# A language-model tower on one core: output products regrouped, and both routers' second products taken over 128 rows

## The reference

```
h = tok(x)                                  # rows of an 8000 x 192 table
h = h + rwkv(layernorm(h))                  # k, v, r = mixed x @ W.T; decayed sums; (sr * y) @ Wo.T
h = h + moe_attention_ffn(layernorm(h))     # router: logits = x @ w_router.T, 4 experts, top 256 of 512 rows each
h = h + ssm_block(layernorm(h))
h = h + experts(layernorm(h))               # router: x @ Wr, 8 experts, top 2, capacity; shared + routed
```

## Time and profile before

| | |
|---|---|
| median of 3 runs | 2166.76 us (2166.21 to 2169.19) |
| the profiled execution: its span, first to last instruction | 2137.2 us |
| the median less that span | 29.6 us |
| TensorE (PE) matmuls busy | 1949.3 us, 91% of the span |
| VectorE (DVE) busy | 1140.4 us, 53% |
| ScalarE (ACT) busy | 739.9 us, 35% |
| GpSimd (POOL) busy | 426.2 us, 20% |
| mean granted TensorE clock | 0.938 |
| the front up to the last copy of logits | 263 us |
| the experts' phase up to its copy of logits | 1365 to 1428 us |

### The profile page before, as it was taken

How to read it: one execution, slowest core, us unless ns; L and a number is a source line. 1 busy time by engine, 2 the same in 40 slices (tenths; PEclk the granted TensorE clock), 3 DMA queues, 4 the chain that set the end, 5 groups by cost and what they waited for, 6 DMA issues and landing times. The chain is left out here.

```text
span 2137.2 us, 28059 instructions
## 1 busy us (share of the span) xinstructions
PE 1949.3 (91%) x10067; PEld 1227.5 (57%) x10075; DVE 1140.4 (53%) x2776; ACT 739.9 (35%) x1248; POOL 426.2 (20%) x567
## 2 busy tenths in 40 slices
PE   4998629999999999879999998799999999999997
PEld 2343523344444544445666665465558888888886
DVE  5798567676667665456877785347322222222221
ACT  1434102544555455544556553121111111111111
POOL 5200111120222021111111111100551222222222
PEclk9988558999999999978999999699999999999999
DMA  2610002111111111000000000200222322122321
GB/s 63 223 50 0 0 18 81 53 52 53 45 53 53 52 45 52 1 31 6 6 6 6 11 6 1 100 1 1 77 95 61 69 60 59 32 62 61 69 38 18
DMA packets 68748, 94.75 MB, mean 44 GB/s; under 512 B 15386, under 2 KB 57662, under 8 KB 66337
## 3 DMA queue, kind: packets, MB, share of 16 engines
q1 hardware_dynamic: 52482, 77.19, 11.2%
q0 software_dynamic: 16128, 15.76, 4.3%
HBM read 54.96 MB, written 39.47 MB: 44 GB/s over the span
## 5 line engine op out<-in xcount | busy, mean ns | idle before, releaser
L1020 DVE TENSOR_REDUCE row_max<-c_ps_m 128x1 f32<-128x512 f32 x384 | 253.1, 686 | 113.8 <-PE c_ps_m L1190 108.5
L1368 ACT ACTIVATE e<-c_ps_s 128x512 f32<-128x512 f32 x384 | 216.5, 596 | 222.2 <-PE c_ps_s L1206 221.5
L2667 DVE TENSOR_TENSOR e_f<-e_ps_u,e_gate 128x512 f32<-128x512 f32 x120 | 83.0, 692 | 271.2 <-ACT e_gate L2949 179.1
L2468 POOL DMA_INDIRECT out<-m_o,m_row_of x80 | 125.7, 1571 | 282.0 <-issue 252.9
L2884 PE MATMUL e_ps_o<-m_w,e_f 128*128 128x192 f32 x960 | 162.6, 326 | 0.9 <-DVE e_f L2667 0.9
L1190 PE MATMUL c_ps_m<-c_kT,qT 96*128 96x512 bf16 x384 | 150.4, 398 | 10.7 <-DVE row_max L1020 10.0
L2884 PEld LDWEIGHTS e_ps_o<-m_w,e_f 128*128 128x128 f32 x960 | 158.1, 190 | 3.3 <-DVE e_f L2667 1.3
L1206 PE MATMUL c_ps_s<-qT,c_kT 97*128 97x512 bf16 x384 | 145.2, 389 | 12.7 <-ACT e L1368 5.3
L2949 ACT ACTIVATE e_gate<-e_ps_g 128x512 f32<-128x512 f32 x120 | 71.6, 597 | 242.3 <-PE e_ps_g L2858 162.3
L2852 PE MATMUL e_ps_g<-m_xT,m_w 128*128 128x256 f32 x480 | 129.6, 392 | 1.0 <-DVE h L2499 1.0
L2852 PE MATMUL e_ps_u<-m_xT,m_w 128*128 128x256 f32 x480 | 123.2, 379 | 0.0
(11 more groups left out here) (458 smaller groups left out, 3725.2 us busy)
## 6 DMA issues: line engine op xcount, KB each, us to landing
dealt<-x SPq DMA_DIRECT2D x8, 1290.0 KB, 15.1
m_x<-dealt SPq DMA_DIRECT2D x40, 258.0 KB, 2.7
spread<-parts SPq DMA_DIRECT2D x24, 384.0 KB, 2.3
qT<-spread SPq DMA_DIRECT2D x144, 64.0 KB, 2.4
c_kT<-spread SPq DMA_DIRECT2D x144, 64.0 KB, 2.5
m_w<-in_w13e SPq DMA_DIRECT2D x8, 1152.0 KB, 5.2
m_w<-in_w2e SPq DMA_DIRECT2D x8, 576.0 KB, 6.2
out<-h SPq DMA_DIRECT2D x8, 384.0 KB, 4.6
```

Of the source, the lines that this page charges most:

```text
L1020: dve.tensor_reduce(row_max[:, n // J, n % J:n % J + 1], ps_m[:, n % 2, :], AX_X, ALU.max)\
L1368: act.activation(e[:, n % LIVE_E, :], ps_s[:, n % 2, :], ACT.Exp, scale=QSCALE).then_inc(e_ready, 1)
L2468: pool.indirect_dma_start(out=out_rows, out_offset=bass.IndirectOffsetOnAxis(ap=row_of[:, n % 2, r:r + 1], axis=0), in_=o[:, n % 2, r, :], ...
L2667: dve.tensor_tensor(fe[:, n % 2, 2 * i:2 * i + 2, :], ps_ue[:, q % 2], gate_e[:, q % 2], ALU.mult)\
```

## The change

`outputs(p)` issues its 8 products over 128 rows first, and the 8 over 64 rows behind them, the two sequences' in turns. Each PSUM bank holds two of the 8 results, so the flag that opens accumulation (`start`) now stands on the first full product of a bank and the one that closes it on the last half product. Both signals of `out_psum` now come behind the last row block. The second product of both routers takes all 128 rows. In the front the added rows of `x1T` are set to zero once, in VectorE's opening, and TensorE waits for that before its first instruction. In the experts' phase the added rows hold the second copy, and their weights are the zeros of the input.

```diff
--- before.py
+++ after.py
@@ -452,6 +452,7 @@
             dve.drain()
             dve.tensor_scalar(row_of[:, :], tok_f[:, :], float(VOCAB), None, ALU.add).then_inc(rows_ready, 1)
             dve.memset(zeros, 0.0).then_inc(zeroed, 1)
+            dve.memset(x1T[HALF:P, :, 1, :], 0.0).then_inc(zeroed, 1)
             dve.memset(xT[:, :, :, 0:1], 0.0)
             dve.memset(omax[:, :, 0:1], NEG_HUGE)
             dve.memset(pnum[:, :, 0:1], 0.0)
@@ -616,17 +617,23 @@
 
             def outputs(p):
                 pe.wait_ge(z_ready, p + 1)
+                if p > 1:
+                    pe.wait_ge(logit_read, p - 1)
                 for u in range(2):
-                    half = slice(u * HALF, (u + 1) * HALF)
                     if p > 0:
                         pe.wait_ge(h_done, 2 * (p - 1) + u + 1)
-                    if p > 1:
-                        pe.wait_ge(logit_read, p - 1)
                     for j in range(J):
                         here = slice(j * P, (j + 1) * P)
-                        pe.matmul(ps_rows[:, u * J + j, 0:C], z[:, 2 * u, here], wo[:, 2 * u, :], start=True, stop=False)
-                        last = pe.matmul(ps_rows[:, u * J + j, 0:C], z[half, 1, here], wo[half, 1, :], start=False, stop=True)
-                    last.then_inc(out_psum, 1)
+                        pe.matmul(ps_rows[:, u * J + j, 0:C], z[:, 2 * u, here], wo[:, 2 * u, :], start=j % 2 == 0,
+                                  stop=False, skip_group_check=True)
+                for j in range(J):
+                    here = slice(j * P, (j + 1) * P)
+                    for u in range(2):
+                        half = slice(u * HALF, (u + 1) * HALF)
+                        last = pe.matmul(ps_rows[:, u * J + j, 0:C], z[half, 1, here], wo[half, 1, :], start=False,
+                                         stop=j % 2 == 1, skip_group_check=True)
+                        if j == J - 1:
+                            last.then_inc(out_psum, 1)
 
             def routed(p):
                 pe.wait_ge(x1_ready, p + 1)
@@ -646,10 +653,11 @@
                         here = slice(j * P, (j + 1) * P)
                         dst = ps_rows[:, u * J + j, C:C + EXPERTS0]
                         pe.matmul(dst, x1T[:, u, 0, here], w_router[:, 0, :], start=True, stop=False)
-                        last = pe.matmul(dst, x1T[0:HALF, u, 1, here], w_router[0:HALF, 1, :], start=False, stop=True)
+                        last = pe.matmul(dst, x1T[:, u, 1, here], w_router[:, 1, :], start=False, stop=True)
                     last.then_inc(logit_psum, 1)
 
             pe.wait_ge(small_in, 80)
+            pe.wait_ge(zeroed, 2)
             turned(0)
             projected("k", 0)
             turned(1)
@@ -2702,7 +2710,7 @@
                 for j in range(J):
                     n, here = (s * J + j) * E8, slice(j * P, (j + 1) * P)
                     pe.matmul(ps_l[:, n:n + E8], xT[:, s, 0, here], wr[:, 0, :], start=True, stop=False)
-                    last = pe.matmul(ps_l[:, n:n + E8], xT[0:HALF, s, 1, here], wr[0:HALF, 1, :], start=False, stop=True)
+                    last = pe.matmul(ps_l[:, n:n + E8], xT[:, s, 1, here], wr[:, 1, :], start=False, stop=True)
                 last.then_inc(logit_psum, 1)
 
             def main(q):
```

## The result

The kernel after took 2140.97 us (median; 2137.13 to 2143.08 in 4 runs) against 2166.49 us before (2165.97 to 2169.19 in 4): a ratio of 0.9874, 95% interval 0.9847 to 0.9901, so 25.5 us faster. The prediction was 2142.6 us.

What follows compares the result with a forecast made beforehand. The front was taken as bound by a chain passing between TensorE and VectorE. Gains of 20.3 us there and 3.9 in the experts' opening, 24.2 off the 2137.2 us span, with 29.6 kept, gave 2142.6 us, range 2133 to 2152.

Steps and rivals of the forecast that it cites:

- The 29.6 us: Whole kernel: the difference between the profiled span before, 2137.2 us, and the timed median, assumed to stay after the change.
- Outputs: Front, output products of one pair: 4.1 to 4.2 us against 8.33 at full clock, 8.0 instead of 14.99 at half.
- Rival 5: Products with equal rows: weight loads run in series with their streams, outputs 8.6 us, kernel slower at 2190 us; chance 0.02.
- Router products: Both routers: without shape changes, products 0.21 us apart instead of 0.32 at full clock, 0.43 instead of 0.51 at half.
- Rival 1: Router products gain nothing, 0.32 us being the pitch of any small product: 2150 us; chance 0.10.
- Path of the front: Front, TensorE and VectorE handing over pair by pair: 18.4 us gained at pair 3's end, 20.3 us in all.
- pair 2: Front: L419 starts 7.5 to 10.2 us earlier, and the second add's end gains 10.7 to 14.1, taken as 12.4.
- Rival 4: Front: TensorE's idle before the router brings half clock, kept until pair 2's outputs; kernel slower at 2174 us; chance 0.03.
- Rival 2: Front outputs: half products don't run side by side, 5.2 us less gain, 2147.8 us; chance 0.07.
- The experts' opening: Eight routers, each 0.8 us shorter; the five where TensorE leads give 5 x 0.8 = 4.0, taken as 3.9 us.
- Sum: Whole kernel: 20.3 us from the front plus 3.9 from the experts' opening, 24.2 us off the profiled span, to 2113.0.

Runs made afterwards that it cites:

- batches of 4: Kernels after and before, with POOL waiting for the scatters' landing after every 4 instead of every 16: 2129.7 and 2154.2 us, against 2182.4 for the unedited kernel before.
- halves in order: Kernel after with all eight half-row products of one sequence issued, then all eight of the other: 2155.8 us, 0.9879 of the kernel before.
- the control: Kernel before, unchanged, run and profiled again: 2171.2 us, 1.0012 of the kernel before.
- only routers: Kernel before with only both routers' second products taken over 128 rows, output products unchanged: 2159.7 us, 0.9952 of the kernel before.
- only outputs: Kernel before with only the output products regrouped, both routers unchanged: 2153.6 us, 0.9912 of the kernel before.
- rolling limit: Kernel after with each scatter waiting for the one four before it, one full wait before the second half: 2105.9 and 2105.2 us on two chips (0.9868, 0.9875).

## Why the prediction came out right, and where it was right for a wrong reason

**The base was misread.** "The 29.6 us that lie between that span and the median are kept": they don't lie around the span, where each run of the kernel after has 1.7 to 1.8 us. The profiled execution of before shows no stall and fits the times of chips C and D (2137.2 + 1.8 = 2139); the timed runs, like those of chip A, fit a chip with it. Subtracting 24.2 from the median still held, because the change doesn't touch the stall, whose length varies by 10 us and more between executions. That the sum came within 1.6 us of the median is luck: the medians of before and after, each pair on one chip, differ by 22.7 us on A, 28.4 on C, 24.5 on B with batches of 4 and 25.5 in the result. Traces without a stall test the sum more directly, though they are single executions and not of one chip: span 2113.0 predicted, 2110.0 on chip C; 24.2 us predicted, 27.2 found.

**Outputs.** 4.1 to 4.2 us predicted, 4.30 measured. Its parts: 8 full products at 0.325 and a change, 2.80 (2.7); halves side by side, 1.50 (1.3 and a change). Per change of shape the outputs paid more than the 0.1 us of the earlier trace rows: with the halves in order 14 changes fewer save 3.3 us, some 0.2 each, the 0.2 us that the prediction had found between 0.52 and 0.325. It put the rest down to weight loads that a change exposes; no run shows that split. At the end 8.0 predicted, 6.70 found, as the clock rose to full within them (mean 0.63). Rival 5, loads in series, is refuted: 4.30 us against its 8.6. So the trace disagrees with the rule of the Trainium skill, "TensorE: Matmul & The Clock Gate", Part 3, that a load overlaps a product only when their row groups differ: loads of 190 ns stand in a stream of one record every 0.175 us. The same part also says that a load aimed at the background weight buffer is pulled ahead, which the prediction didn't weigh; the trace is in keeping with that, though it doesn't show which buffer a load goes to.

**Router products.** 0.21 predicted, 0.22 to 0.23 found; at half clock 0.43 and 0.43, so pair 1's router 6.81 for 6.9 (it took 6.11 before, partly at full clock). Rival 1 is refuted by the same rows.

**Path of the front.** Predicted 20.3 us. Outputs(0) start anywhere from 92.3 to 94.7 us, ahead of any edit but the memset, so the front is best counted from there. It lasts 168.2 us in the trace of before and in the control, and 144.9 to 147.9 in the eight traces with the whole change: 20.3 to 23.3 us, and 20.3 for the two traces of chip A. The place of the half clock makes most of the spread. The kernel after on A had half clock all through its last transposes and router, and took 10.75 us for the 7.22 of the first trace (length, busy; clock; DMA share; GB/s):

```profile
231.00:241.75 10.75, 10.33 (x49) 0.50 0.01 2
```

It touches the kernel before as well. With batches of 4, which leave the front alone, its front took 164.0 us. Pair 1's outputs ran at full clock there, and in the trace of before (first row) mostly at half:

```profile
137.73:150.86 13.13, 13.13 (x33) 0.59 0.06 27
137.33:145.67 8.34, 8.34 (x33) 1.00 0.06 26
```

So some 4 us of the front's gain are there only when the kernel before loses the clock at that place, as it did in the other two traces of it and in only routers (13.1 us).

Step by step in the trace after, whose outputs(0) start 2.4 us earlier than the sum had them: the second adds end at 98.5, 143.1, 186.7 and 222.9, for 101, 146, 187 and 225. With those 2.4 us taken out, the gains are 3.2, 6.4, 10.1 and 17.6 us, for 3.2, 6.2, 12.4 and 18.4. The step that was mis-sized is pair 2. L419 starts 7.0 us earlier and not 7.5 to 10.2 (9.4 with the 2.4). The prediction let the router of pair 1 start at the second add's end; it starts 1.1 us behind it, at 144.22, for it waits for ScalarE's copy of `b_xT`, which stands behind the exponentials; it ran at half clock throughout, and k(3) takes 10.91 us (11.15). At the end the outputs of pair 3, 8.3 us shorter for 7.0, gave a part of it back, and the last transposes and router the rest. Rival 4, a clock kept down, is refuted: k(3) started at half clock after 5.8 us of idle and a router at half clock, and full clock was back within it, mean 0.85.

**Rival 2** (halves not side by side, 5.2 us) is refuted by the pairs of records that start together. Its price for pair 0, 1.3 us, is what 16 records 0.16 us apart would cost; no run kept the halves wholly apart, and the one that did so in part lost 0.5 us in the front, so what the overlap is worth in time was not measured.

**The experts' opening.** 3.9 predicted, 5.2 found, in every kernel with the second edit, and the size hides two errors. Here is how far TensorE of the kernel after is ahead, counted from the first transposes of each trace (us), with its wait for ScalarE ahead of the transposes behind a router, before and after (behind router 8 the copy of the logits is taken):

| router | ahead at its start | wait, before and after | ahead behind it | gained at it |
|---|---|---|---|---|
| 1 | 0.00 | none | 0.76 | 0.76 |
| 2 | 1.98 | 0.29, 0.95 | 1.97 | 0.0 |
| 3 | 2.02 | none, 0.76 | 1.84 | -0.2 |
| 4 | 3.42 | none, 0.22 | 3.77 | 0.35 |
| 5 | 3.78 | 0.56, 1.21 | 3.78 | 0.0 |
| 6 | 3.78 | 0.30, 0.95 | 3.79 | 0.0 |
| 7 | 3.78 | none | 4.52 | 0.74 |
| 8 | 4.53 | none | 5.1 | 0.6 |

Routers 2, 5 and 6 gave nothing, as predicted: what each lost came back as a wait, 0.65 us more than before. But of the five that TensorE led, two had almost no slack. The step that failed is "5 x 0.8 = 4.0, less little where the slack is just used up": the five gave 2.3 us. The other 2.8 are between routers, where no instruction changed. They are the clock. The stretch from router 1 to router 2 and that from router 3 to router 4, before and then after:

```profile
1373.21:1381.68 8.47, 8.47 (x21) 0.65 0.14 58
1392.39:1398.56 6.17, 6.17 (x22) 0.72 0.00 1
1345.70:1352.95 7.25, 7.25 (x21) 0.77 0.26 107
1363.80:1368.39 4.59, 4.59 (x21) 1.00 0.00 2
```

In the kernel after the first half-clock stretch ends 10.5 us behind the first transposes and not 13.8, and a third one, some 3 us long, is missing. The control, only outputs and the kernel after on A and C show the same pattern to 0.04 us, so it belongs to the kernels and not to an execution. That the shorter router moves the clock is shown by only routers, which has the 56.8 us without the other edit; the prediction's sum had no such term here, and allowed 2 or 3 us either way for the whole kernel. Its total for the opening was near by luck.

**Sum.** 27.2 found without a stall, less 24.2: the opening was 1.3 short, the front about 1, and 0.9 fell between them, in phases that no edit touches (they take 1098 to 1103 us in the fourteen traces).

## What to carry to other kernels

Products of alternating shape pay at each change of array shape: about 0.1 us in this kernel's routers of 4 or 8 columns, some 0.2 in its outputs of 192 columns. Group them by shape, or fill the short one with zeros; at full clock a record of 192 columns then took some 0.16 us and a tiny one 0.11. Before adding a predicted gain to a median, compare the profiled execution's own time with the timed runs: a gap of 1% is a different execution, and its place in the trace is to be found by profiling the kernel before again. Judge a change at landmarks ahead of any stretch that varies, not by spans. And follow a loop step by step before its total is explained: here more than half of a gain that looked like seven routers in eight was a shorter time at half clock.

## What the runs showed that I had not expected

On chips A and B, and in the trace of the result, ScalarE and VectorE stand still again and again while POOL issues row scatters back to back (one every 1.28 us), although TensorE has ended what they wait for; the longest stands are 17 to 30 us. In all six such traces VectorE's first long one ends within 1 us of the end of POOL's first pause (some 2.3 us, for the landing of a batch) and ScalarE's within 2, while later ones end at a pause in some and between pauses in others. In sum the stretch is 29 to 49 us longer; on C it isn't, and the times of D speak against it there. With a pause after every 4 scatters it is gone, here at the price of 20 us of waiting for the rows. The trace gives "remote" as the releaser, so the signal that came late is not in it; the scatters' own packets keep their distance from their issue, to 0.1 us, with and without a stall. What holds the signals back stays open: a limit on unlanded scatters and POOL's unbroken issuing are both still possible, and so is whether the rolling limit, free on chips without the stall, removes it on the others. Of the complete kernels run, the best on chip B was the kernel after with batches of 4 (0.976 of before; the unedited kernel after was not run there); on C and D it was the kernel after, with or without the rolling limit.
